# Two-layer attention and expert kernel: maxima's products twelve units ahead, four rounds to a step

## The reference

```
sim     = einsum('bhqd,bhkd->bhqk', q / sqrt(16), k)   # 2 batches, 16 heads, 512 queries
weights = softmax(sim with masked keys at -inf or -1e9)
out     = einsum('bhqk,bhkd->bhqd', weights, v)        # then, in layer 0, out @ Wo.T + bo
x       = x + out
```

## Time and profile before

| | us |
|---|---|
| timed runs, median of 3 | 596.76 |
| lowest and highest | 594.78, 597.42 |
| span of the profiled execution | 601.6 |
| PE busy | 554.9 (92%) |
| DVE busy | 259.3 (43%) |
| ACT busy | 208.8 (35%) |
| L714 on PE, 512 products | 100.1 busy |
| L725 on PE, 256 products | 98.3 busy |
| L878 on DVE, 128 reductions | 84.9 busy |

### The profile page before, as it was taken

The page is one execution under the profiler, slowest core; times in us unless marked ns, Lnnn a source line. Parts: engine busy times, 40 slices in busy tenths (PEclk is TensorE's granted clock), DMA queues, the critical chain, the costliest instruction groups (busy, mean ns, idle before and its releaser), DMA issues.

```text
span 601.6 us, 8029 instructions
## 1 busy us (share of the span) xinstructions
PE 554.9 (92%) x2865; PEld 362.5 (60%) x2867; DVE 259.3 (43%) x766; ACT 208.8 (35%) x393; POOL 84.6 (14%) x124
## 2 busy tenths in 40 slices
PE   2998999889889999798699989999999999999995
PEld 1456455554678888665344444665667676767663
DVE  5375777552247463473646543252222221222120
ACT  1444444442446552235533463321112112211221
POOL 2300600022102100200000000007212112211222
PEclk9997999996999999659879898999999999999998
DMA  8400006992112220393000006202672112211211
GB/s 304 139 1 0 1 2 220 367 354 104 36 35 89 73 86 27 128 369 124 2 0 1 2 0 218 71 1 99 199 254 34 32 26 36 32 31 27 36 17 25
DMA packets 38783, 54.17 MB, mean 90 GB/s; under 512 B 3341, under 2 KB 32461, under 8 KB 38736
## 3 DMA queue, kind: packets, MB, share of 16 engines
q1 hardware_dynamic: 29552, 40.07, 19.9%
q0 software_dynamic: 4336, 6.75, 5.7%
q10 hardware_dynamic: 4848, 6.76, 3.4%
HBM read 39.05 MB, written 14.51 MB: 89 GB/s over the span
## 4 chain that ended last, share of the span: by engine, by line
PE 85%; DVE 7%; ACT 4%; DMA 2%; issue 2%; POOL 0%; SPq 0%; DVEq 0%; POOLq 0%; ACTq 0%
PE PS L1670 16%; PE PS L714 10%; PE PS L725 9%; PE PS L1695 8%; PE PS L742 6%; PE PS L1594 5%; PE PS L1471 4%; PE PS L1482 4%; PE PS L300 4%; PE PS L320 4%; PE PS L1605 3%; PE PS L1683 2%; PE PS L289 2%; PE PS L732 2%; DVE W L878 2%
## 5 line engine op out<-in xcount | busy, mean ns | idle before, releaser
L878 DVE TENSOR_REDUCE W<-PS 128x2 f32<-128x512 f32 x128 | 84.9, 686 | 70.2 <-PE PS L714 69.5
L714 PE MATMUL PS<-W 32*128 32x256 f32 x512 | 100.1, 442 | 7.2 <-ACT W L576 5.3
L725 PE MATMUL PS<-W 32*128 32x512 f32 x256 | 98.3, 706 | 1.7 <-ACT W L970 1.3
L1670 PE MATMUL PS<-W,PR 128*128 x304 | 97.9, 466 | 0.0
L714 PEld LDWEIGHTS PS<-W 32*128 32x128 f32 x512 | 65.7, 207 | 41.0 <-issue 20.4
L1670 PEld LDWEIGHTS PS<-W,PR 128*128 128x128 f32 x304 | 54.9, 190 | 30.2 <-issue 6.0
L1695 PE MATMUL PS<-W,PR 128*128 x228 | 56.1, 388 | 0.7 <-DVE PR L1716 0.7
L1695 PEld LDWEIGHTS PS<-W,PR 128*128 128x128 f32 x228 | 41.7, 189 | 15.0 <-issue 7.3
L2398 POOL DMA_INDIRECT out<-PR,slots x19 | 29.5, 1555 | 144.3 <-ACT PR L2343 117.4
L970 ACT ACTIVATE PR<-PS 128x512 f32<-128x512 f32 x64 | 35.2, 597 | 22.8 <-PE PS L725 22.6
L970 ACT ACTIVATE W<-PS 128x512 f32<-128x512 f32 x64 | 34.9, 598 | 23.1 <-PE PS L725 23.1
(11 more groups left out here) (262 smaller groups left out, 694.4 us busy)
## 6 DMA issues: line engine op xcount, KB each, us to landing
W<-in_L_ffn_W SPq DMA_DIRECT2D x16, 512.0 KB, 9.9
W<-in_rguT SPq DMA_DIRECT2D x5, 1408.0 KB, 10.3
W<-in_rdT SPq DMA_DIRECT2D x5, 640.0 KB, 11.4
W<-in_mask SPq DMA_DIRECT2D x3, 1024.0 KB, 14.0
scratch_rows<-W SPq DMA_DIRECT2D x1, 2860.0 KB, 14.7
W<-in_rguT ACTq DMA_DIRECT2D x2, 1408.0 KB, 11.0
VR<-scratch_rows SPq DMA_DIRECT2D x19, 130.0 KB, 2.0
scratch_x<-W SPq DMA_DIRECT2D x1, 2048.0 KB, 14.2
```

Of the source, the lines that this page charges most:

```text
L714: m = pe.matmul(PS[:, u % 3, q * FK:(q + 1) * FK], QT[r:r + 32, g, c:c + 128], KT[r:r + 32, g, b * FK:(b + 1) * FK], start=True, stop=True)
L725: pe.matmul(PS[:, 3 + u % 3, :], KT[r:r + 32, g, b * FK + kb * 128:b * FK + (kb + 1) * 128], QT[r:r + 32, g, 512 * b:512 * (b + 1)], start ...
L878: dve.tensor_reduce(NM[:, s % 2, q:q + 2, c], PS[:, u % 3, :].rearrange("p (q n) -> p q n", q=2), AX, ALU.max).then_inc(sem("m_free"), 1)
L1670: m = pe.matmul(PS[:, b0 + hf, 0:352], XS[:, r % 2, k, :], W[:, bass.ds(slot * SLOT + o, 352)], start=(k == 0), stop=(k == 1))
```

## The change

A layer's first part (`pe_first`, `dve_first`) now computes twelve score units instead of eight, and turns the maxima of step 0 there. A step is four rounds (`rounds`): round r of step s has score units 12 + 8s + 2r and the next one, which belong to steps s + 1 and s + 2, and weight units 2r and 2r + 1. `WEIGHTS` orders the weight units so that a round's two scores and two weights use four different quarters. Between the rounds stand the whole-array pieces: outputs after round 0, the turned outputs after round 1, the turned maxima of step s + 1 after round 2. Where `halved` says so, the outputs' first half (keys 0 to 127) stands after round 3 of the same step, and only the second after round 0 of the next. In layer 1, steps 2 and 3 have rounds of their own, since the second batch's queries come late. Turning and projecting are cut in halves, one to a bank; those of layer 1's second batch begin one step earlier. Other work moves to the new places, and the list of bank users with it. VectorE and ScalarE follow; the statistics of layer 0's rows are taken from the fifth unit of step 5 on.

```diff
+    WEIGHTS = (2, 3, 0, 1, 6, 7, 4, 5)
+    FIRST = 12
+
+    def rounds(l, s):
+
+        if (l, s) == (1, 2):
+            return [([28, 29], [0, 1]), ([30, 31], [2, 3]), ([], [4, 5]), ([], [6, 7])]
+        if (l, s) == (1, 3):
+            return [([], [0, 1, 2, 3]), (list(range(32, 40)), []), ([40, 41], [4, 5]), ([42, 43], [6, 7])]
+        u = FIRST + 8 * s
+        return [([n for n in (u + 2 * r, u + 2 * r + 1) if n < 64], [2 * r, 2 * r + 1]) for r in range(4)]
+
+    def halved(l, s):
+
+        return (l, s) not in ((0, 1), (0, 2), (1, 0)) and s < 7
...
+    def pe_round(l, s, r):
+        scores, weights = rounds(l, s)[r]
+        for n in range(max(len(scores), len(weights))):
+            if n < len(scores):
+                pe_scores(l, scores[n])
+            if n < len(weights):
+                pe_weights(l, s, weights[n])
 
     def pe_step(l, s):
-        more = s < 7
-        if more:
-            pe_scores(l, s + 1, 0)
-            pe_scores(l, s + 1, 1)
-        if (l, s) == (0, 5):
-            pe.wait_ge(sem("wp_3"), 16)
-            project_batch("project0", "close0", 3, 0)
-        pe_turn_max(l, s)
         if (l, s) == (0, 7):
             taken(6, "rows0_0")
+            taken(7, "rows0_0")
             pe.wait_ge(sem("wgc"), 2)
             logits_pe(0, 0, 4, 2).then_inc(sem("logits_ps"), 1)
-        if l == 0 and s == 1:
-            pe.wait_ge(sem("vals"), 4)
+        pe_round(l, s, 0)
         if s:
-            pe_outputs(l, s - 1)
-        for i in range(4):
-            if more:
-                pe_scores(l, s + 1, 2 + i)
-            pe_weights(l, s, i)
-            if i == 1:
-                pe_beside(l, s, 1)
+            for kb in range(halved(l, s - 1), 2):
+                pe_outputs(l, s - 1, kb)
+        pe_beside(l, s, 0)
+        pe_round(l, s, 1)
         if s:
             pe_turn_out(l, s - 1)
+        pe_beside(l, s, 1)
+        pe_round(l, s, 2)
+        if s < 7:
+            pe_turn_max(l, s + 1)
+        pe_beside(l, s, 2)
+        pe_round(l, s, 3)
         pe_beside(l, s, 3)
...
+        if halved(l, s):
+            pe_outputs(l, s, 0)
...
+    def dve_step(l, s, v, late, beside=lambda r: None):
+        for r in range(4):
+            scores, _ = rounds(l, s)[r]
+            for u in scores:
+                dve_top(l, u)
                 next(late, None)
...
+            if r == 0 and l == 0 and s < 2:
                 mask_keys(0, 2 + s)
+            if r == 1 and s:
+                dve_divide(l, s - 1, v)
+            if r == 2 and s < 7:
+                dve_add_max(l, s + 1)
+            beside(r)
...
+        def rows_counted():
+            for _ in range(4):
+                yield
+            yield from aggregates(v, COLUMN["rows0_0"], rows_of(0))
...
+        def second_rows():
+            for _ in range(4):
+                yield
+            dve.wait_ge(*full_free(6, "q1_1"))
+            dve.wait_ge(*full_free(7, "q1_1"))
+            yield from statistics(v, "q1_1", [RW[:, j, :] for j in range(4)])
```

More of the change, by code:

```diff
@@ L236, in bank_uses @@
+    def halved(l, s):
+        return (l, s) not in ((0, 1), (0, 2), (1, 0)) and s < 7
     def bank_uses():
         six, seven = [], []
[L238 to L241, removed]
+        beside = {(0, 0, 3): [("wg", 7)], (0, 1, 3): [("count0", 67)], (0, 2, 3): [("count1", 67)],
[5 rows of a table added]
@@ L242, in bank_uses @@
         after = (["close1", "project1", "rows0_1", "x1_0", "q1_0"], ["rows1_1"])
         for l in range(NB):
+            seven.append(("max", l, 0))
             for s in range(8):
[L245 to L254, removed]
+                for e in range(4):
+                    if e == 0 and s and not halved(l, s - 1):
+                        six.append(("outputs", l, s - 1))
+                    if e == 1 and s:
+                        seven.append(("turned", l, s - 1))
+                    if e == 2 and s < 7:
+                        seven.append(("max", l, s + 1))
+                    for name, banks in beside.get((l, s, e), []):
+                        if banks != 6:
+                            seven.append(name)
+                        if banks != 7:
+                            six.append(name)
+                    if e == 3 and halved(l, s):
+                        six.append(("outputs", l, s))
@@ L751, in pe_turn_out, with turn_half, project_half @@
         filled(7, m)
+    def turn_half(use, rows, k):
+        claim(6 + k, use)
+        filled(6 + k, turn4(6 + k, rows, k))
+    def project_half(use, before, wi, b, k):
+        claim(6 + k, use)
+        taken(6, before)
+        taken(7, before)
+        for j in (2 * k, 2 * k + 1):
+            m = projected(6 + k, j, wi, XT, 512 * b + 128 * j)
+        filled(6 + k, m)
     def turn_batch(use, rows):
@@ L823, in pe_first @@
             pe.wait_ge(*at(0, "qt", 4))
[L824 to L827 removed]
+            for u in range(8):
+                pe_scores(0, u)
+                if u % 2:
+                    queries_second(u // 2)
             pe.wait_ge(*at(0, "qt", 8))
@@ L899, in add_projected @@
             freed(6 + j, dve.tensor_tensor(xj, xj, PS[:, 6 + j, :].rearrange("p (t c) -> p t c", c=D), ALU.add))
-        for j in range(2):
+        for j in halves:
             dve.wait_ge(sem(f"free{6 + j}"), USES[6 + j][use])
@@ L1775, in fast_pe @@
             pe_step(0, s)
-        pe_outputs(0, 7)
+        for kb in range(2):
+            pe_outputs(0, 7, kb)
         pe.wait_ge(*at(1, "wp_1", 16))
@@ L1840, in second_pe @@
             pe_step(1, s)
-        pe_outputs(1, 7)
+        for kb in range(2):
+            pe_outputs(1, 7, kb)
         pe.wait_ge(sem("rowsT_1"), 2)
```

285 lines of the change are left out of this document (138 added, 147 removed), and 5 rows, old and new, of the table beside.

## The result

| | before | after |
|---|---|---|
| timed, median (4 runs each) | 597.09 us | 580.37 us |
| ratio, with its 95% interval | | 0.9738 (0.9697 to 0.978) |
| profiled execution, span | 601.6 us | 581.0 us |
| its mean granted clock | 0.943 | 0.939 |

A forecast was written before the change was run, and what follows sets the result against it. TensorE's sequence in the two attention stretches was taken as the bound: 33.0 us of schedule gain less 6.6 for half clock gives 26.4 off the 596.76 median, 570.4 us; own range 563 to 579, whole range 557 to 586.

The forecast's parts named there:

- Clean steps: Attention steps without extra work: 8.0 us against 9.72, from 7.5 of pieces and 0.5 of waits; sign 7.8 to 8.5.
- rounds: Two score and two weight units on four row quarters: 1.09 us each; sign 1.1 to 1.35 to the next piece.
- steps 2 and 3 of layer 0: VectorE, also counting keys, becomes the bound: 10.7 and 10.3 us, from 12.32 and 10.35.
- Step 5 of layer 1: Some 4 us more VectorE work (statistics, sum of outputs): 10.8 us, from 13.13.
- Step 3's stretch of scores alone: Layer 1: eight score units alone, set by VectorE, 5.2 us instead of 2.2; the step 15.15.
- The logits: Step 7 of layer 0: 1.35 us, taken as half of today's 2.7 at half clock.
- The waits: TensorE waits 2.5 us before the rows in layer 0's step 6 and 3.1 in layer 1's step 2.
- The clock: Half clock for about 7 us in each layer, after waits with light work behind; 6.6 us lost.
- Taking the gain off the median: The profiled span's gain of 26.4 us was taken unchanged off the timed median of 596.76.
- Banks (584): Banks not yet free cost 0.4 us in each of 49 rounds with scores; 13.7 us lost; chance 0.17.
- Layer 0 handed back: Scatter, gather and weights bound the first expert tile; some 8 of layer 0's 14 us lost, 578; chance 0.08.
- The slow rival: Half clock through most of both attention stretches, as whole-array visits empty the array: 645 us; chance 0.04.

The follow-up runs named there:

- Experiment 6: Changed kernel with weight units in order 0, 1, 2, ..., so a round's scores and weights share row quarters; 649.38 us, ratio 1.0611 to before.
- experiment 1: Changed kernel plus eight thrown-away projections on TensorE before the wait for normalized rows in layer 0's step 6; 578.95 us, ratio 0.9597 to before.
- experiment 5: Changed kernel with the next layer's first pair of key projections moved from step 7 into layer 0's step 6 wait; 570.3 us, ratio 0.9578 to before.
- experiment 3: Changed kernel with layer 1 step 3's 12 score units spread four each over rounds 1 to 3; 586.21 us, ratio 0.9789 to before.
- experiment 10: Changed kernel with both pairs of key projections earlier, in step 6's wait and behind step 7's logits and outputs; 573.07 us, ratio 0.9568 to before.
- experiment 4: Changed kernel with the outputs nowhere cut in halves, both behind round 0 of the next step; 578.09 us, ratio 0.9661 to before.
- experiment 8: Changed kernel with outputs nowhere cut and the first pair of key projections in step 6's wait; 575.69 us, ratio 0.9649 to before.
- experiment 11: The changed kernel run again, nothing altered; 582.64 us, ratio 0.9672 to before.
- experiment 12: Changed kernel with first key pair in step 6's wait, plus thrown-away products in layer 1 step 2's wait; 572.55 us, ratio 0.9577 to before.

## Why the prediction was right, and where it missed

By its own steps, in us, at the marks of the profile:

| | predicted | measured |
|---|---|---|
| layer 0, steps 0 to 5 | 60.5 | 58.5 |
| layer 0, steps 6 and 7 | 23.2 | 35.9 |
| layer 1, steps 0 and 1 | 25.15 | 24.5 |
| layer 1, steps 2 and 3 | 26.4 | 31.2 |
| layer 1, steps 4 to 7 | 36.75 | 34.1 |
| sum (before 205.1) | 172.0 | 184.2 |

- **Clean steps, rounds, steps 2 and 3 of layer 0**: right, but for one wait. The round between whole-array pieces is 1.08 us (1.09 forecast). A step 4 has turned rows or queries beside it: 8.96 us came in layer 0 (8.9 forecast) and 8.64 in layer 1 (8.85), the latter just over the 7.8 to 8.5 that the prediction named as its sign. The barest step is step 5 of layer 1: 8.59 us, 7.5 of products as forecast and 1.1 of waits where 0.5 was forecast. The missing part is the wait of the turned maxima, which "wait for nothing any more" in the prediction: they wait 0.83 us there for the bank that VectorE's division frees. Steps 2 and 3 took 11.08 and 9.99 (10.7 and 10.3 forecast) with VectorE busy 9.96 and 9.30. Experiment 6 shows that the quarters carry the gain.
- **Step 5 of layer 1**: missed. It was given 10.8 for VectorE's extra work; it took 8.59, with VectorE busy 7.96.
- **Step 3's stretch of scores alone**: right. It is 5.5 us in experiment 1, and the step takes 15.83 nearly at full clock, against 15.15.
- **The logits**: misread. The prediction took half of today's 2.7 us as their full-clock time, 1.35. But half clock began at 133.3 in that profile, 1.0 us behind their start at 132.29, so the 2.7 were a mixture. At full clock they take 1.95 us (experiments 1 and 5), 0.6 more.
- **The waits**: right in kind. 1.93 us came in step 6 (2.5 forecast). In step 2 of layer 1 (3.1 forecast) 1.49 came ahead of the maxima, and 0.99 ahead of the queries where TensorE had run at full clock until then (experiments 3 and 10); in the changed kernel's profile slower products covered that one.
- **The clock: this term was mis-sized.** I took off 6.6 us for 7 us at half clock in each layer. The profile has 27.3 and 13.6. What they cost follows from the same steps at nearly full clock. Steps 6 and 7 took 23.57 us in experiment 10, 25.3 with the wait that it fills, so 10.7 of the 35.9 are the clock's. Step 3 lost 2.9 (18.69 less 15.83) and step 2 lost 1.3 (12.48 less 11.16). That is 14.9 instead of 6.6. The prediction took each fall for the consequence of a wait. Experiment 1 shows a fall with no wait, and experiment 4 idle times of 1.43 and 0.83 us with no fall in or right behind them. Experiments 5, 8 and 10 show that at the end of layer 0 the half clock gets shorter when the same work is put in another order (13.7, 3.4 and 3.4 us). What decides when the clock falls stays open.
- **The work itself** came out 2.7 better than forecast: 33.0 + 2.7 - 14.9 = 20.8, the 20.6 of the spans and the 0.2 of the stretches around. Most of the 2.7 is luck with the clock too: step 0 of layer 0 was forecast at 9.9 with 6.5 us of half clock and took 8.19 at full clock. In experiment 11, the same kernel with that half clock, it took 10.1.
- **Taking the gain off the median**: also wrong. The profiled run of before had 68.6 us at half clock, its 25 runs a mean of 53.3. The forecast had counted on getting 31 us of it back, and in the usual run less of it was there. The changed kernel's profile had 70.9, which is usual for it (mean 69.9). So the 20.6 of the profiles, both near 70, is 16.7 on the medians. At equal clock the change is worth 23 us, and 17 us more at half clock give 7 of them back.
- **Rivals.** Banks (584) would show as rounds over 1.5 us to the next piece. Of the 40 rounds of four units that stand alone at full clock, 33 are under that, 21 of them at 1.10 or less. Six of the other seven stand ahead of the turned maxima (1.55 to 2.80 us, with the wait for VectorE in it), one takes 1.62. All waits together are some 0.2 us a round, between the forecast's 0.12 and the rival's 0.4: a part of that rival came true. Layer 0 handed back: the stretch behind it grew by 1.7 us, no more. Both kernels wait 1.8 us for VectorE at the first expert tiles there; only the changed one has 3.4 us of half clock behind that wait. Experiment 5 moved the end of step 7 by 6 us and kept it. The slow rival did not come.

So the gain of the schedule came as forecast, and the time is 10.0 us behind it: inside the whole range of 557 to 586, just outside the forecast's own 563 to 579. 8.3 of the ten are the clock's term and 3.9 the step from the profiles to the medians; 2.7 came back from work priced too high, most of that by step 0's clock and not by insight.

## What to carry to other kernels

Price the clock as a term of its own, from several runs, before a gain that rests on one profile is taken off a median: here a microsecond at half clock cost 0.42. Then look at waits and at light stretches behind them (lone units on part of the array, logits, transposes) as places where dense work can be put: moving two real projections into a wait, with no work added, brought ten microseconds, of which eight were clock. Try such a move in more than one place, since in layer 1 it only shifted the fall (experiment 12). Units that are to run side by side must stand on different row quarters. Lead and order together decide that, and where they clash a round more than doubles.

## What was not expected

- The clock fell with TensorE busy 17.98 of the 18.08 us before (experiment 1).
- Seven microseconds of filler, thrown away, cost the kernel nothing: 578.95 against 580.37 and 582.64. At equal clock it is 5.6 us behind; 22 us less at half clock paid for it.
- Score and weight products on shared quarters take 2.46 us for what takes 1.08 side by side, more than the 1.9 of two product times.
- One and the same step 3 took 15.8, 18.7 or 22.8 us, with 1.2, 8.8 and 20.2 us of it at half clock.
- Idle times of 1.43 and 0.83 us close together did not lower the clock (experiment 4), where one of 1.93 was followed by 27.3 us at half clock.
